# First block of each layer gathered whole, and nodes in runs of 125 over partitions, in a two-layer graph kernel

## What is computed

```python
# layer 0
ew  = (efeat @ W_e + b_e).reshape(E, 16, 16)
msg = einsum('ei,eio->eo', feat[src], ew)
neigh = segment_sum(msg, dst) / maximum(count, 1) + bias
x = layernorm(x + neigh)
# layer 1
msg = einsum('emh,eh->em', edge_emb[edge_type].reshape(-1, 16, 16), x[src])
m = segment_sum(msg, dst)
h_new = GRU(m, x)            # gates: sigmoid, sigmoid, tanh
x = layernorm(x + h_new)
```

## Time and profile before

| | |
|---|---|
| median of the runs | 5046.9 us (3 runs, 5046.0 to 5047.23) |
| the profiled execution, its own time | 5047.75 us, span 5045.9 us |
| busy | PE 93%, DVE 85%, PE weight loads 78%, POOL 73%, ACT 68% |
| layer 0 in steady state | one block each 20.0 us |
| layer 1 in steady state | one block each 18.7 us |
| a gather on POOL | 0.944 us, and 0.30 until the next |
| a pick on PE | 8 matmuls, 1.5 us at full clock |
| a select on DVE | 0.57 + 0.57 us for one column, 0.99 + 0.99 for two |
| an outer product, 8 columns | 2.28 us in layer 0, 1.22 in layer 1 |
| one-hots of one third on ACT | 4.04 us (3 columns) |

### The profile page before, as it was taken

The page is one execution under the profiler, slowest core; times in us unless marked ns, Lnnn a source line. Parts: engine busy times, 40 slices in busy tenths (PEclk is TensorE's granted clock), DMA queues, the critical chain, the costliest instruction groups (busy, mean ns, idle before and its releaser), DMA issues.

```text
span 5045.9 us, 118005 instructions
## 1 busy us (share of the span) xinstructions
PE 4685.8 (93%) x33412; PEld 3960.1 (78%) x33413; DVE 4267.2 (85%) x5536; ACT 3446.3 (68%) x6806; POOL 3668.7 (73%) x3883
## 2 busy tenths in 40 slices
PE   5999999999999999999969999999999999999997
PEld 4777777777777777777758888888888888888886
DVE  6988988988998998898958888888888888888886
ACT  5766666666666666666647777777777777777772
POOL 4777777777777777777746777777777777777773
PEclk9999999999999999999979999999999999999997
DMA  3212222222212212221211111111111121111110
GB/s 68 33 33 35 33 33 35 33 33 34 33 33 33 34 33 32 35 33 32 35 28 23 27 26 27 27 27 26 27 27 27 26 27 27 27 26 27 27 26 15
DMA packets 403225, 153.40 MB, mean 30 GB/s; under 512 B 228186, under 2 KB 402186, under 8 KB 403065
## 3 DMA queue, kind: packets, MB, share of 16 engines
q1 hardware_dynamic: 279190, 120.96, 11.9%
q0 software_dynamic: 124000, 31.99, 7.9%
HBM read 150.03 MB, written 2.56 MB: 30 GB/s over the span
## 4 chain that ended last, share of the span: by engine, by line
POOL 41%; issue 28%; DVE 11%; DMA 9%; PE 5%; ACT 2%; DVEq 1%; SPq 1%; POOLq 0%; ACTq 0%
POOL z L376 41%; DVE cand L642 5%; PE psN L504 4%; DMA z<-h_rows,idx 3%; DVE z L671 3%; DMA idx<-in_src 3%; DMA z<-in_x,idx 2%; DVE nodeT L628 1%; ACT pick L420 1%; PE psN L596 1%; ACT dist L414 1%; DVEq L627 0%; DVE z L646 0%; PE psN L576 0%; SPq L266 0%
## 5 line engine op out<-in xcount | busy, mean ns | idle before, releaser
L504 PE MATMUL psN<-table_hi,pick 128*128 128x400 f32 x9500 | 3380.7, 356 | 177.0 <-DVE cand L642 116.7
L504 PE MATMUL psN<-table_lo,pick 128*128 128x400 f32 x9500 | 3272.5, 344 | 0.0
L376 POOL DMA_INDIRECT z<-in_x,idx x2000 | 1893.7, 947 | 659.1 <-issue 586.8
L376 POOL DMA_INDIRECT z<-h_rows,idx x1875 | 1774.0, 946 | 644.5 <-issue 537.0
L504 PEld LDWEIGHTS psN<-table_hi,pick 128*128 128x128 f32 x9500 | 1786.1, 188 | 484.9 <-issue 409.9
L420 ACT ACTIVATE pick<-dist,one 128x384 fp32r<-128x384 f32 (+1 forms) x3000 | 1719.7, 621 | 212.2 <-PE psN L504 212.2
L504 PEld LDWEIGHTS psN<-table_lo,pick 128*128 128x128 f32 x9500 | 1789.9, 188 | 0.1
L414 ACT ACTIVATE dist<-src_mod,neg_node 128x384 f32<-128x384 uint16 (+1 forms) x3000 | 1722.3, 622 | 24.2 <-DMA src_mod<-src_mod_rows 24.2
L646 DVE TENSOR_REDUCE z<-cand 128x16 f32<-128x400 f32 (+1 forms) x1375 | 1199.9, 873 | 116.0
L642 DVE TENSOR_TENSOR cand<-psN,grp_hot 128x400 f32<-128x400 f32 (+1 forms) x1375 | 1197.6, 871 | 85.3 <-PE psN L504 62.3
L671 DVE TENSOR_TENSOR z<-psD,z 128x1024 f32<-128x1024 f32 (+1 forms) x564 | 923.1, 1637 | 313.5 <-DMA z<-h_rows,idx 248.6
(11 more groups left out here) (103 smaller groups left out, 811.5 us busy)
## 6 DMA issues: line engine op xcount, KB each, us to landing
src_mod<-src_mod_rows SPq DMA_DIRECT2D x625, 96.0 KB, 3.0
z<-in_x,idx POOLq DMA_INDIRECT x2000, 2.4
z<-h_rows,idx POOLq DMA_INDIRECT x1875, 2.4
eab<-in_edge_attr SPq DMA_DIRECT2D x125, 200.0 KB
src_mod<-src_mod_rows SPq DMA_DIRECT2D x125, 128.0 KB
idx<-in_src SPq DMA_DIRECT2D x250, 12.5 KB
dstb<-in_dst SPq DMA_DIRECT2D x250, 14.0 KB
grp<-src_grp SPq DMA_DIRECT2D x250, 5.0 KB
```

The source lines that it names most:

```text
L376: pool.indirect_dma_start(xs[k][buf][:, g, :], None, table, bass.IndirectOffsetOnAxis(ap=idx[buf][:, g:g + 1], axis=0),).then_inc(l["got"] ...
L504: mm = pe.matmul(psN[:, bank(buf, t), 0:NG * F], pick[j][:, c, at:at + P], table_p[part][:, c * NG * F:(c + 1) * NG * F], start=(c == 0 an ...
```

## The change

1. **Block 0 is gathered whole** in both layers: POOL issues all 25 columns, and the picks, one-hots, selects and mask of block 0 go away on PE, ACT and DVE, with its source loads on SP. The semaphores start with the counts that these would have given. PE's waits for the split table and the weights move into the first body. In layer 1 DVE's split stands behind the first outer product.
2. **SP's order** at the start: spans are written and read back, weights loaded, and only then the sources of block 1. h is loaded in layer 0 after the last edge loads, and bias is added to it after the aggregation.
3. **Node n sits on partition n % 125, column n // 125**: a column of nodeT is 125 elements in a run, and DMAs of h, h_dram and the output move runs of 64 bytes.
4. **Between the layers** DVE takes each group of 25 columns through all steps (row_sums, normalise), ACT takes the root by group, and SP stores each group as it is ready; POOL waits for all eight stores. SP issues layer 1's first loads behind group 0's store.
5. **At the end** the last steps of the GRU run over 20 columns at a time with the row sums in them, and the output goes in two halves, on SP's queue and on ACT's.

```diff
...
 NS = len(START) - 1
+N_LN = 4
 PICKED = [5, 6, 7, 13, 14, 15, 21, 22, 23, 24]
...
+        def ln_cols(g):
+            return slice(g * (C // N_LN), (g + 1) * (C // N_LN))
+
         def cols(t, c):
-            return t[:, c:N:C]
+            return t[:, c * R:(c + 1) * R]
+
+        def by_node(rows):
+            return rows.rearrange("(c r) f -> r c f", r=R)
+
+        def got_of(k, buf, j, r):
+            return 16 * (len(GATHERED[k][j]) * (r + 1) + (PCUT[k][j + 1] - PCUT[k][j] if buf == 0 else 0))
...
-            def node_rows(out_t, in_t, s):
+            def node_rows(out_t, in_t, cs, s):
                 for a, b in ((0, n16), (n16, R)):
-                    sp.dma_start(out_t[a:b], in_t[a:b]).then_inc(s, 16)
+                    sp.dma_start(out_t[a:b, cs], in_t[a:b, cs]).then_inc(s, 16)
...
                     for j in range(NS):
-                        sp.wait_ge(l["got"][buf][j], 16 * len(GATHERED[k][j]) * (r + 1))
+                        sp.wait_ge(l["got"][buf][j], got_of(k, buf, j, r))
                         sp.wait_ge(l["pick_act"], TC * (NS * b + j + 1) + 1)
...
             sp.dma_start(grp_dram, src_rows).then_inc(s_modd, 16)
-            sp.wait_ge(s_modd, 32)
-            for b in range(2):
-                load_src(0, b, b)
             sp.wait_ge(s_span, 1)
...
             sp.dma_start(bias_b[:], bias[0, :].partition_broadcast(R)).then_inc(s_w, 16)
-            node_rows(h[:], x.rearrange("(r c) f -> r c f", c=C), s_w)
+            sp.wait_ge(s_modd, 32)
+            load_src(0, 1, 1)
             edge_loads(0)
-            sp.wait_ge(s_h, 1)
-            node_rows(h_dram.rearrange("(r c) f -> r c f", c=C), yb, s_hd)
-            for b in range(2):
-                load_idx(1, b, b)
-                load(1, b, b)
-                load_src(1, b, b)
-            sp.wait_ge(s_hd, 32)
+            node_rows(h[:], by_node(x), slice(0, C), s_x)
+            for g in range(N_LN):
+                sp.wait_ge(s_h, g + 1)
+                node_rows(by_node(h_dram), yb, ln_cols(g), s_hd)
+                if g == 0:
+                    for b in range(2):
+                        load_idx(1, b, b)
+                        load(1, b, b)
+                    load_src(1, 1, 1)
+            sp.wait_ge(s_hd, 32 * N_LN)
             load_table(1, h_dram)
...
             sp.wait_ge(s_out, 1)
-            node_rows(out.rearrange("(r c) f -> r c f", c=C), yb, s_done)
-            sp.wait_ge(s_done, 32)
+            node_rows(by_node(out), yb, slice(0, C // 2), s_done)
+            sp.wait_ge(s_done, 64)
         N_TAB = 16 * (TC + -(-(N % GRP) // P))
-        N_W = 13 * 16
+        N_W = 11 * 16
...
-                def body(b, buf, r):
+                def body(b, buf, r, whole=False):
                     pool.wait_ge(l["idx"][buf], 16 * (r + 1))
...
                     for j in range(NS):
-                        for g in GATHERED[k][j]:
+                        for g in range(START[j], START[j + 1]) if whole else GATHERED[k][j]:
                             pool.indirect_dma_start(
...
                             ).then_inc(l["got"][buf][j], 16)
-                for_each_block(pool, body)
+                body(0, 0, 0, whole=True)
+                with pool.Fori(0, (NB - 1) // 2) as i:
+                    body(2 * i + 1, 1, i)
+                    body(2 * i + 2, 0, i + 1)
...
             gathers(0, x)
-            pool.wait_ge(s_hd, 32)
+            pool.wait_ge(s_hd, 32 * N_LN)
             gathers(1, h_dram)
...
                     n, lo, hi = TC * (NS * b + j), PCUT[k][j] * P, PCUT[k][j + 1] * P
-                    act.wait_ge(l["src"][buf][j], 16 * (r + 1))
+                    act.wait_ge(l["src"][buf][j], 16 * (r + buf))
                     for c0 in range(0, TC, 2):
...
                     h_to_rows()
-                for b, j in ((0, 0), (0, 1), (0, 2), (1, 0), (1, 1)):
-                    pick_third(b, b, 0, j)
-                if k == 0:
+                else:
                     copy_coef(0, 0, 0)
+                for j in range(2):
+                    pick_third(1, 1, 0, j)
                 if k == 0:
...
                     act.wait_ge(s_ht, g + 1)
-                    v = nodeT[0:2 * F, 0:N].rearrange("f (r c) -> f c r", c=C)[:, 4 * g:4 * g + 4, :]
-                    act.copy(v, psN[0:2 * F, g % 4, 0:4 * R].rearrange("f (c r) -> f c r", r=R)).then_inc(s_hc, 1)
+                    act.copy(nodeT[0:2 * F, 4 * g * R:4 * (g + 1) * R], psN[0:2 * F, g % 4, 0:4 * R]).then_inc(s_hc, 1)
...
             evacuate(0)
-            act.wait_ge(s_var, 1)
-            act.activation(st[2][:], st[1][:], ACT.Sqrt, bias=eps[:, 0:1], scale=1.0 / F).then_inc(s_a, 1)
+            for g in range(N_LN):
+                act.wait_ge(s_var, g + 1)
+                act.activation(st[2][:, ln_cols(g)], st[1][:, ln_cols(g)], ACT.Sqrt, bias=eps[:, 0:1], scale=1.0 / F).then_inc(s_a, 1)
             evacuate(1)
...
                 act.activation(ya[:, cs, :], ya[:, cs, :], ACT.Tanh).then_inc(s_n, 1)
-            act.wait_ge(s_var, 2)
-            act.activation(st[2][:], st[1][:], ACT.Sqrt, bias=eps[:, 0:1], scale=1.0 / F).then_inc(s_a, 1)
+            act.wait_ge(s_var1, 1)
+            act.activation(st[2][:], st[1][:], ACT.Sqrt, bias=eps[:, 0:1], scale=1.0 / F).then_inc(s_a1, 1)
+            act.wait_ge(s_out, 2)
+            for a, b in ((0, R // 16 * 16), (R // 16 * 16, R)):
+                act.dma_start(by_node(out)[a:b, C // 2:C], yb[a:b, C // 2:C]).then_inc(s_done, 16)
...
                             if not (isinstance(b, int) and b + 1 >= NB):
+                                if t == 0:
+                                    pe.wait_ge(s_split, k + 1)
                                 pick_rows(b + 1, 1 - buf, t)
                             if t == 0:
+                                if k == 0:
+                                    pe.wait_ge(s_w, N_W)
                                 flush_result(first)
...
-                pe.wait_ge(s_split, k + 1)
-                for t in range(H[k]):
-                    pick_rows(0, 0, t)
                 if k == 0:
-                    pe.wait_ge(s_w, N_W)
                     pe.wait_ge(s_meta, 1)
...
-                    dve.wait_ge(l["grp"][buf], 16 * (r + 1))
+                    dve.wait_ge(l["grp"][buf], 16 * (r + buf))
                     dve.tensor_tensor(grp_hot[:, 0:H[k], :], col_f[:, 0:NG].unsqueeze(1).to_broadcast([P, H[k], NG]),
...
                     cs, m = slice(START[j], START[j + 1]), START[j + 1] - START[j]
-                    dve.wait_ge(l["got"][buf][j], 16 * len(GATHERED[k][j]) * (r + 1))
+                    dve.wait_ge(l["got"][buf][j], got_of(k, buf, j, r))
                     dve.wait_ge(l["sel"], H[k] * b + PCUT[k][j + 1])
...
-                dve.wait_ge(s_tab[k], N_TAB)
-                rows = table[:].rearrange("p c g f -> p c f g")
-                hi, lo_part = (t[:].rearrange("p (c f g) -> p c f g", c=TC, f=F) for t in table_p)
-                step(dve.tensor_copy(hi, rows))
-                step(dve.tensor_tensor(lo_part, rows, hi, ALU.subtract))
-                dve.sem_inc(s_split, 1)
+                def split_table():
+                    dve.wait_ge(s_tab[k], N_TAB)
+                    rows = table[:].rearrange("p c g f -> p c f g")
+                    hi, lo_part = (t[:].rearrange("p (c f g) -> p c f g", c=TC, f=F) for t in table_p)
+                    step(dve.tensor_copy(hi, rows))
+                    step(dve.tensor_tensor(lo_part, rows, hi, ALU.subtract))
+                    dve.sem_inc(s_split, 1)
+
                 if k == 0:
+                    split_table()
                     before_blocks()
-                group_hot(0, 0, 0)
                 match_block(0, 0, 0)
-                for t0, t1 in sum(PAIRS[k], ()):
-                    select(0, 0, t0, t1)
+                outer(0, 0, 0, 0)
+                if k == 1:
+                    split_table()
                 group_hot(1, 1, 0)
-                outer(0, 0, 0, 0)
                 for_each_block(dve, body, peeled=3)
...
-            def centre_and_square():
-
-                step(dve.tensor_scalar(st[0][:], st[0][:], 1.0 / F, None, ALU.mult))
-                step(dve.tensor_tensor(yb[:], ya[:], bc(st[0], F), ALU.subtract))
-                step(dve.tensor_tensor(ya[:], yb[:], yb[:], ALU.mult))
-                step(dve.tensor_reduce(st[1][:], ya[:], AX.X, ALU.add))
-                dve.sem_inc(s_var, 1)
-
+            def row_sums(cs):
+                step(dve.tensor_reduce(st[0][:, cs], ya[:, cs, :], AX.X, ALU.add))
+                step(dve.tensor_scalar(st[0][:, cs], st[0][:, cs], 1.0 / F, None, ALU.mult))
+                step(dve.tensor_tensor(yb[:, cs, :], ya[:, cs, :], bc(st[0][:, cs], F), ALU.subtract))
+                step(dve.tensor_tensor(ya[:, cs, :], yb[:, cs, :], yb[:, cs, :], ALU.mult))
+                step(dve.tensor_reduce(st[1][:, cs], ya[:, cs, :], AX.X, ALU.add))
...
                 dve.sem_inc(l["free"], 1)
```

(56 more changed lines are left out.)

## The result

| | before | after |
|---|---|---|
| median of the runs | 5046.84 us (5046.0 to 5047.23) | 5004.76 us (5002.55 to 5006.33) |
| ratio, 95% interval | | 0.9917 [0.9899, 0.9934] |
| profiled execution, span | 5045.9 us | 5003.6 us |
| busy | PE 93%, DVE 85%, POOL 73%, ACT 68% | PE 93%, DVE 85%, POOL 74%, ACT 68% |

The change makes the kernel 42.1 us (0.83%) faster; 48.8 were forecast. First the page of the profile after: its chain of waits.

What follows compares the result with a forecast made beforehand. POOL's gathers bound it, each layer a fixed number of gathers behind its restart. Layer 0's start -27.5, layer 1's start -18.8 and tail -2.5 sum to -48.8; 5047.75 - 48.8 - 0.85 = 4998.1 us, range 4982 to 5013.

Steps and rivals of the forecast that it cites:

- What bounds the kernel: Whole kernel: POOL's gathers run without pause, 1.249 us each, so moving a restart moves the end one for one.
- Start of layer 0: Layer 0 up to POOL's restart: block 0 free at 69.5 instead of 97.01, -27.5 us, between -23 and -31.
- Rest of layer 0: Layer 0 after the restart: keeps its gathers, and the moved load of h costs nothing.
- Between the layers: From aggregation's end A to layer 1's first gather: POOL starts at A + 31.3 instead of A + 40.1.
- The prediction's own branch for 0.23: Transposes between the layers: at 0.23 us each, the normalised rows end at A + 29.7 instead of A + 25.8.
- Start of layer 1: Layer 1's restart: POOL itself last after 40 gathers, A + 84.4 instead of A + 103.2, -18.8 us, between -22 and -13.
- Tail: After the last gather: gates gain 3.3 us, last store issued earlier but takes longer; -2.5 us, between -5 and +9.
- (1): Contiguous weights change nothing: +4 us between the layers, +3 in the tail, 5005; chance 0.14.
- (2): PE's clock rises to 2.4 GHz in the tail, DVE then limits: about -17 us, 4981; chance 0.09.
- (3): Short writes at twice the read price: +8.2 us at the end, +4.1 between the layers, 5010; chance 0.17.
- (4): Short writes at five times today's price per run and engine make it slower than before: 5055 and above; chance 0.03.
- (5): Block 1's picks hold block 0, and its 25 gathers delay layer 1: only some 18 us remain, 5029; chance 0.07.

Runs made afterwards that it cites:

- seven rows of the table: The kernel before, the changed kernel and five variants of either, cut at the same points; medians from 5046.8 us (before) to 4991.3 us.
- the sources first: Changed kernel with gate operands zero-filled to 128 partitions and layer 0's block 1 sources loaded ahead of the eleven weight loads: 4991.33 us.
- 128 rows: Changed kernel with the gates' two operands filled up from 48 to 128 partitions by zeros: 4996.13 us.
- the whole gather alone: Kernel before with block 0 of each layer gathered whole and nothing else changed: 5017.60 us.
- the old order: Changed kernel with the nodes numbered as before, strided in SBUF, long rows in DRAM: 5000.32 us.

## Why the prediction was right, and which terms were off

- **What bounds the kernel**: right. The steady part is the same within 0.5 us in layer 0 and 1.1 in layer 1 in all seven rows of the table, and each gain at a restart is one at the end. The 6.5 us by which -48.8 missed -42.3 are 2.3 at the start, 0.9 up to A, 1.8 in layer 1 and its lead-in, and 1.5 in the tail.
- **Start of layer 0**, -27.5 forecast, -25.2 measured. The whole gather was free as said: its 41 gathers end at 59.65 (forecast 59.7). The outer product's start was forecast late, by 2.1 us. The step that was too cheap is that of the picks, "PE has block 1's sixth pick at 59", priced at 1.5 each: it left out that block 0's own sums need two copies which ACT has queued behind two thirds, and that matmuls are slow again after the pause. The 68.19 with the sources first shows the price of both: 3.6 us, in one execution of each; between the medians of the two kernels over 128 rows it is 4.8.
- **Rest of layer 0**: h at nothing, right (-0.2). The 1.1 us from the last gather to A was in no term. Its cause is open: PE's granted clock is 0.50 there and 0.66 in the same stretch of before, but the kernel with 128 rows and the sources first takes 12.2 us at 0.64, and the whole gather alone 11.2 at 0.65.
- **Between the layers**, POOL's start at A + 31.3 forecast, A + 34.6 measured. The term that was mis-sized is the transposes': "With 0.18 or less DVE sets the pace, and I take that". They took 0.212, DVE waited 1.56 and 0.77 us for them, and the rows were ready at A + 28.6 for 25.8. The contiguous weights were priced without the clock; the two runs with 128 rows show 0.105 at the high clock, and the range of 0.1 to 0.23 held both. The prediction's own branch for 0.23 was exact: the rows are ready at A + 29.8 with the old order, for A + 29.7. The store took 6.1 us behind them for 5.5.
- **Start of layer 1**: the mechanism was right. POOL itself is last (block 0 was free at about A + 83.6), and 40 gathers and the split's 2.8 us take what was said; A + 87.4 for A + 84.4 is the late start, 3.3, and little else. Another 1.1 us was gained in the steady part behind it, which no term has and no run explains. That the early h and the whole gather share their gain, 15.8 for 22.0, follows from the same: with both, POOL's own 40 gathers are the limit.
- **Tail**, -2.5 forecast, -1.0 measured. Line 616 gained the 3.3, a size that was right for a wrong reason. The reason given, that the 128 moving columns set 0.211 whatever the weights do, doesn't hold: with the old order it is 0.231 again. The last store is first issued 8.3 us earlier, for 8.4 forecast; the miss is the store, 11.9 us for 10.5.
- **Rivals.** (1), contiguous weights change nothing: wrong, but closer between the layers than the forecast, 0.212 against 0.231. Its total, 5005, is the one measured to 0.3 us, and that is luck: line 616 has the 3.3 us that it denies, and other terms than its own, 2.3 at the start and 1.4 in the last store among them, make up the distance. (2), the clock rises by itself: no, 0.50 for 43 us. Its price of 17 was also too high: its own terms, 43 less 5 x 5.7, give 14.5, and where the clock was made to rise the tail fell by 10.1. (3), short writes at twice the price of short reads: no, 92 GB/s against the 114 of the earlier trace rows. The Trainium skill (DMA: Bandwidth & Descriptors, Specifications) wants 512 bytes or more; by direction the runs agree, 11.9 us for 5.1, by the short rows alone. (4) and (5) no.

The prediction spoke of the change as a whole and let its parts 3 and 4 share one sum. Taken apart, the node order gained 3.4 us in the gates and 1.9 in the transposes (ACT's shorter copies are hidden), and cost 6.9 in the last store and 3.0 in the store of h; 1.2 of the 1.9 reach POOL's first gather of layer 1, where the balance was 1.8 against it, and at the end it was 3.8. The order by itself thus lost time, inside a change that won 42.

## What to carry to other kernels

A first step that needs nothing prepared (here a whole gather on an idle queue, 29 of the 42 us when put in alone) can be worth more than a speed-up of what prepares it, but its gain ends where that queue itself becomes last: count its own instructions first. In a stretch where one engine waits for a tiny step of another, look at what that step is queued behind, and at the clock after the pause. And a layout has a price on each side: here the one that halves a weight load at the high clock makes 12,500 DMA rows out of 250. At the low clock it lost 3.8 us in the tail, at the high one it won 7.1.

## What the runs showed of the hardware

- Gates over 48 partitions, with PE busy for 42.4 of 43 us, stayed at a granted clock of 0.50 (1.2 GHz) in every kernel here and on both chips; over 128, of which 80 hold zeros, the clock went to 1.00 (2.4 GHz) in all four executions, with contiguous and with strided weights. Matmuls over 128 partitions with 17 moving columns for 128 stayed at 0.50 with PE busy for 40.0 of 40 us. Transposes over 17 partitions that began at 1.00 were at 0.50 some 2 us later, without a pause, in two executions. What decides between these cases was not tried.
- A matmul with its weight load of 125 f32 columns with a step of 400 bytes takes 0.231 us at either clock, with 17 as with 128 moving columns; contiguous it is 0.21 at 1.2 GHz and 0.105 at 2.4. The Trainium skill (SBUF — State Buffer, the cacheline note) says that each access to a new 16-byte line pays; the runs agree, and here the strided time didn't shrink with the clock.
- ACT writing 500 f32 columns with that step took 1100 ns, contiguous 582.
- 12,500 writes of 64 bytes to DRAM, from two queues, took some 7 us more than 250 long ones: 92 GB/s over 8 us, against 160 over the 5 us of the long rows. The store of h between the layers took 6.1 us from its last rows to POOL's first gather with rows of 64 bytes, 3.05 with long ones.
- One chip granted a mean clock of 0.78 with pauses on PE and ran the same kernel in 8368 us; a kernel with little slack on PE can have another bound there.
